# Moving the epsilon, the scale and the shift of four norms from GpSimd to VectorE in a two-layer vision tower

## The chip, the cores and the metric

The kernel runs on one core of one Trainium2 chip. The metric is device time in microseconds of one execution; the time given is the median of three runs. Engines are named as the profile names them: PE is TensorE's matmul, PEld its weight load, DVE is VectorE, ACT is ScalarE, POOL is GpSimd, SP is the queue that issues the transfers.

## The reference, cut to what matters

Thirty-two images of 3x96x96 become 37 tokens each (36 patches and a class token) of 256 numbers, 1184 tokens in all. Two layers follow, each with an attention-like part and a feed-forward part, and each part reads a layer norm of the residual `h`:

```
h = tok(x)                                             # patches @ W + b, class token, positions
h = h + minlstm(norm(h))                               # its own second norm, gates, scan over tokens, + its input
h = h + ffn(norm(h))                                   # ternary W_fc, gelu, norm over 1024, ternary W_proj
h = h + attention(norm(h))                             # rope, causal softmax, V and output weights
h = h + quant_linear(norm(h))                          # round(x / scale), clip, ternary weights
norm(h) = (h - mean) / sqrt(var + 1e-5)
```

The first part norms twice in a row; the kernel folds that into the powers of two numbers, `var + eps` and `var * (1 + eps) + eps * eps`. In the last part the normed value is divided by `scale = max(act_scale, 1e-5)` before rounding.

## The kernel before, in words

The 1184 tokens are cut into 11 tiles of three images, 111 rows each (74 in the last), one token to a partition. Each tile passes through the stages `tok`, `gate`/`scan`/`h1`, `fc`/`tg`/`proj`, `qk`/`value`/`score`/`attend`, and `t3`/`out`. `gate`, `scan`, `qk` and `rope` work on chunks of 4, 4 and 3 tiles. Matmuls in float32 are done as products of a high and a low part, so a PE result that is to be multiplied again is copied by ACT (high part) and subtracted by DVE (low part).

The order of work is written out by hand: the table `ORDER` holds for each engine a list of steps `stage:tile` (`stage:unit` for chunked stages), which the engine's program issues one after the other. Engines meet only at semaphores. The PSUM banks are handed out in the order of PE's list (`ring`), so moving a PE step also changes which earlier result a bank waits for. `NARROW`, with two banks, is shared by `w_pos`, `tok`, `h1`, `proj`, `value`, `score`, `attend`, `out` and some weight steps.

Each of the norms 0 to 3 of a tile is computed from one row of `small`, 35 numbers per token:

- DVE, `stats0` to `stats3` (L885): `bn_stats` of the 256 numbers of a row; `mean0` to `mean3` (L892): `bn_aggr`, giving mean and variance (`MV`), which raises `mv`.
- POOL, in its steps `h0` (norm 0), `h1` (norm 1), `proj` (norm 2) and `attend` (norm 3): `scaled` (L1181) computes `var + eps` into `VE`; norm 0 has two such instructions. `power` (L1186) raises to -0.5 into `R`, against the constant tile `powers`. Norm 3 multiplies by `1/scale` (L1272) into `RQ`. Norms 1 to 3 then have `shift` (L1191), which writes `-mean * R` into `NB`. Between any two of them POOL waits for its own semaphore. Norm 0's shift is already on DVE (L990).
- ACT, `n0` to `n3` (L729): `h * R + NB`. For norm 3 this is `s3`, which DVE clips (L1146) and rounds (L1154) and PE transposes (`t3`, L653) and multiplies (`out`, L664).

POOL's other work is: `split` (L1202, the low part of the input), `square` (the power of the 1024-wide norm, L1186 too), `hc`, `vbias` and `biased` (L1233, L1260, L1282, a 256-wide bias added to the residual), and `rope` (L1251). At the start SP issues the loads in the order input tile 0, `w_tok` in two halves, input tile 1, `pos_in` and `sel`, input tile 2 and so on; `w_pos` (L440) is the small matmul that needs `pos_in` and `sel`, and `warm` (L435) is a row of matmuls on ones.

Of the kernel before, what the change touches and what calls it, by code (L numbers as in the profile page):

```python
# [20 lines left out]
ALU = mybir.AluOpType  # L21
# [46 lines left out]
def chunk_of(i):  # L68
# [7 lines left out]
        warm:0 tok:0 w_pos:0 tok:1 tok:2 tok:3 w_gate:0 tok:4 t0:0 tok:5 t0:1 tok:6 t0:2 tok:7 w_fold:0 t0:3  # L76
        w_ternary:0 t0:4 w_fold:1 tok:8 tok:9 gate:0 gate:1 t0:5 w_value_bias:0 gate:2 gate:3 t0:6 tok:10 t0:7
        w_ln_bias:0 gate:4 gate:5 h1:0 gate:6 h1:1 t0:8 t0:9 h1:2 t0:10 gate:7 h1:3 t1:0 gate:8 gate:9 fc:0 t1:1
        fc:1 h1:4 gate:10 h1:5 h1:6 gate:11 h1:7 fc:2 t1:2 fc:3 t1:3 tg:0 fc:4 fc:5 tg:1 fc:6 fc:7 t1:4 tg:2
        tg:3 proj:0 h1:8 fc:8 t1:5 fc:9 tg:4 tg:5 fc:10 proj:1 h1:9 tg:6 fc:11 t1:6 t1:7 proj:2 h1:10 tg:7 fc:12  # L80
        tg:8 fc:13 tg:9 t2:0 fc:14 proj:3 t1:8 fc:15 tg:10 t2:1 tg:11 fc:16 proj:4 t2:2 tg:12 proj:5 t2:3 tg:13
        t1:9 fc:17 qk:0 qk:1 fc:18 tg:14 tg:15 proj:6 t1:10 qk:2 tg:16 qk:3 proj:7 t2:4 tg:17 fc:19 fc:20 t2:5
        value:0 t2:6 proj:8 fc:21 score:0 t2:7 tg:18 score:1 tg:19 qk:4 qk:5 score:2 turn:0 tg:20 proj:9 qk:6
        score:3 attend:0 tg:21 qk:7 value:1 turn:1 t2:8 proj:10 t2:9 value:2 attend:1 turn:2 value:3 score:4
        attend:2 turn:3 score:5 score:6 t2:10 attend:3 score:7 turn:4 qk:8 qk:9 qk:10 value:4 t3:0 turn:5
# [1272 lines left out]
```

## Time and profile before

| | us |
|---|---|
| median of 3 runs (163.96 to 165.28) | 164.39 |
| the profiled execution's own time | 163.71 |
| its span, first to last instruction | 161.9 |
| PE busy | 148.2 |
| DVE busy | 136.1 |
| POOL busy | 120.3 |
| ACT busy | 109.0 |

Times of rows are from the start of the span. Busy time is the union of an engine's instructions, and on PE an instruction's end is modelled, so PE can be "busy" over short waits. The profiled execution is 0.68 us under the median of the runs. The line numbers are those of the kernel before.

### The profile page before, as it was taken

To read this page: it belongs to the slowest core of one execution; us is meant where nothing else is said; L and a number is where in the kernel's file an instruction comes from. 1 tells how busy PE (TensorE), PEld (TensorE's weight loads), DVE (VectorE), ACT (ScalarE), POOL (GpSimd) and SP (SyncE) were. 2 spreads that over 40 slices of the span, in tenths; PEclk is the share of its full clock that TensorE was granted. 3 is DMA by queue.
4 is the path that set the end of the run, shared out by engine and by line. 5 is a ranking of instruction groups with operands and counts; after the bars stand their busy time and mean duration, and the time that the engine had idled before them with its cause. 6 is when DMAs were issued, how large, how long until landed. Compare 5 with 4: busy or idle time off the path is not lost.

```text
span 161.9 us, 3532 instructions
## 1 busy us (share of the span) xinstructions
PE 148.2 (91%) x1043; PEld 129.5 (80%) x1043; DVE 136.1 (84%) x396; ACT 109.0 (67%) x264; POOL 120.3 (74%) x214
## 2 busy tenths in 40 slices
PE   7979999999998999999999999999999999697541
PEld 7969999788997887879888989988998798574220
DVE  0767679999999999999979799888988896896871
ACT  3765359736448899999998958498827637276330
POOL 1068978968927466878889988869899888988830
PEclk9999999999999999999999999999999999999955
DMA  5999992000030000000000000000000000001323
GB/s 171 340 392 392 379 417 109 4 0 2 0 130 4 2 0 2 0 4 0 0 4 2 0 4 0 2 0 0 4 0 0 0 6 2 2 10 46 87 81 81
DMA packets 6026, 10.84 MB, mean 67 GB/s; under 512 B 1841, under 2 KB 3448, under 8 KB 5752
## 3 DMA queue, kind: packets, MB, share of 16 engines
q1 hardware_dynamic: 6008, 10.62, 18.7%
q8 instruction: 9, 0.15, 0.4%
q14 instruction: 9, 0.07, 0.2%
HBM read 9.40 MB, written 1.21 MB: 66 GB/s over the span
## 4 chain that ended last, share of the span: by engine, by line
PE 70%; POOL 13%; DVE 6%; issue 6%; ACT 2%; DVEq 0%; ACTq 0%; POOLq 0%
PE bank L428 37%; PE bank L508 5%; PE bank L575 5%; PE bank L509 4%; PE bank L510 4%; PE bank L517 3%; POOL small L1186 3%; PE bank L435 3%; POOL qk L1251 2%; POOL small L1181 2%; POOL residual L1282 2%; POOL small L1191 2%; PE bank L549 1%; PE bank L629 1%; DVE residual L1160 1%
## 5 line engine op out<-in xcount | busy, mean ns | idle before, releaser
L1186 POOL TENSOR_TENSOR small<-small,powers 111x1 f32<-111x1 f32 (+3 forms) x55 | 33.3, 606 | 3.7
L1181 POOL TENSOR_SCALAR small<-small 111x1 f32<-111x1 f32 (+1 forms) x55 | 24.2, 441 | 15.0 <-DVE small L892 11.3
L428 PE MATMUL bank<-pj,gt_hi 128*111 128x256 f32 (+1 forms) x88 | 22.3, 293 | 0.0
L428 PE MATMUL bank<-pj,gt_lo 128*111 128x256 f32 (+1 forms) x88 | 21.3, 281 | 0.0
L1202 POOL TENSOR_TENSOR x_lo<-x_raw,x_hi 128x666 fp32r<-128x666 f32 (+1 forms) x9 | 12.8, 1434 | 10.8 <-ACT x_hi L721 10.8
L508 PE MATMUL bank<-wt_hi,x_hi 128*111 128x256 f32 (+1 forms) x66 | 19.4, 294 | 1.4 <-DVE h L998 1.1
L510 PE MATMUL bank<-wt_hi,x_lo 128*111 128x256 f32 (+1 forms) x66 | 18.6, 282 | 0.0
L509 PE MATMUL bank<-wt_lo,x_hi 128*111 128x256 f32 (+1 forms) x66 | 18.6, 282 | 0.0
L428 PE MATMUL bank<-fc,n1t_hi 128*111 128x512 f16 (+1 forms) x44 | 16.7, 380 | 0.0
L428 PE MATMUL bank<-fc,n1t_lo 128*111 128x512 f16 (+1 forms) x44 | 16.6, 378 | 0.0
L428 PEld LDWEIGHTS bank<-pj,gt_hi 128*111 128x111 f32 (+1 forms) x88 | 15.1, 171 | 0.3 <-DVE residual L1088 0.2
L428 PEld LDWEIGHTS bank<-pj,gt_lo 128*111 128x111 f32 (+1 forms) x88 | 15.1, 171 | 0.1
L815 ACT ACTIVATE gt_hi<-bank 128x444 fp32r<-128x444 f32 (+1 forms) x22 | 11.7, 537 | 4.4 <-PE bank L575 4.2
L1111 DVE SCALAR_TENSOR_TENSOR rope<-bank,packed,consts 128x444 f32<-128x444 f32 (+1 forms) x24 | 13.4, 621 | 1.2 <-PE bank L428 1.1
L1071 DVE SCALAR_TENSOR_TENSOR gw<-g,small,ln_w 111x1024 f32<-111x1024 f32 (+1 forms) x11 | 14.3, 1296 | 0.0
L897 DVE TENSOR_TENSOR gt_lo<-bank,gt_hi 128x444 fp32r<-128x444 f32 (+1 forms) x22 | 13.1, 596 | 1.2 <-ACT gt_hi L815 1.2
L885 DVE BATCH_NORM_STATS2 stats<-residual 111x6 f32<-111x256 f32 (+1 forms) x33 | 13.9, 420 | 0.2
L729 ACT ACTIVATE n<-residual,small 111x256 f32<-111x256 f32 (+1 forms) x22 | 13.3, 604 | 0.6 <-POOL small L1191 0.6
L508 PEld LDWEIGHTS bank<-wt_hi,x_hi 128*111 128x111 f32 (+1 forms) x66 | 11.5, 174 | 2.6 <-DVE h L998 1.5
L1251 POOL TENSOR_TENSOR qk<-rope 128x444 f32<-128x444 f32 (+1 forms) x12 | 13.0, 1108 | 0.7 <-DVE rope L1111 0.5
L795 ACT ACTIVATE g<-bank 111x512 f32<-111x512 f32 (+1 forms) x22 | 13.1, 605 | 0.4 <-PE bank L428 0.3
L1191 POOL TENSOR_SCALAR small<-small 111x1 f32<-111x1 f32 (+1 forms) x33 | 10.7, 325 | 3.4
(139 smaller groups left out, 478.9 us busy)
## 6 DMA issues: line engine op xcount, KB each, us to landing
x_raw<-x_in SPq DMA_DIRECT2D x10, 333.0 KB, 6.4
w_fc<-w_fc_in SPq DMA_DIRECT2D x1, 1024.0 KB, 10.2
w_pj<-w_pj_in SPq DMA_DIRECT2D x1, 1024.0 KB, 12.2
out_dram<-residual SPq DMA_DIRECT2D x10, 96.0 KB, 1.7
w_tok<-w_tok_in SPq DMA_DIRECT2D x2, 384.0 KB, 4.1
w_gate<-w_gate_in SPq DMA_DIRECT2D x1, 512.0 KB, 5.8
w_qk<-w_qk_in SPq DMA_DIRECT2D x1, 512.0 KB, 7.0
ln_w<-ln_w_in SPq DMA_DIRECT2D x1, 512.0 KB, 3.5
```

The costliest lines, as they stand in the source:

```text
L428: last = mm(out, a, b, start=(n == 0), stop=(n == len(pairs) - 1))
L508: mm(out[0:n, 0:D], hi, wt_hi[:, k, :], start=(k == 0), stop=False)
L509: mm(out[0:n, 0:D], hi, wt_lo[:, k, :], start=False, stop=False)
L510: last = mm(out[0:n, 0:D], lo, wt_hi[:, k, :], start=False, stop=(k == KX - 1))
L729: return go(out, h[0:n, i, :], ACT.Identity, scale=small[0:n, i, factor:factor + 1], bias=small[0:n, i, shift:shift + 1])
L885: nc.vector.bn_stats(stats[0:n, norm, i % 2, 0:6], h[0:n, i, :]).then_inc(s[f"stats{norm}_ready"], 1)
L1071: stt(out=gw[0:n, i % 2, :], in0=g[0:n, i % 2, :], scalar=col(i, MVG), in1=ln_w[0:n, :], op0=ALU.subtract, op1=ALU.mult).then_inc(s["gw_re ...
L1111: last = stt(out=rope[:, t, 0:width].rearrange("p (m t) -> p m t", t=T), in0=banks[WIDE[("qk", 4 * c + b)][0]][:, 0:width].rearrange("p (m ...
L1181: return nc.gpsimd.tensor_scalar(small[0:rows(i), i, out:out + 1], small[0:rows(i), i, value:value + 1], factor, add, ALU.mult, ALU.add)
L1186: return gt(small[0:rows(i), i, r:r + n], small[0:rows(i), i, ve:ve + n], powers[0:rows(i), 0:n], ALU.pow)
L1191: nc.gpsimd.tensor_scalar(small[0:rows(i), i, nb:nb + 1], small[0:rows(i), i, mv:mv + 1], small[0:rows(i), i, r:r + 1], -1.0, ALU.mult, AL ...
L1251: gt(qk[:, 2 * j + part, cs], rope[:, t, 0:width], rope[:, t + 1, 0:width], op)\
```

## The change

On DVE, `mean0` to `mean3` get a second part: after `bn_aggr` they wait for its own semaphore and compute `VE` (two instructions for norm 0, one for norms 1 and 2). For norm 3 the one instruction computes `(var + eps) * scale^2`, so the power gives `R/scale` directly; the multiplication by `1/scale` is gone, and the reciprocal in `w_small` becomes a square. New DVE stages `nb1`, `nb2`, `nb3` wait for POOL's power and compute `NB`. POOL's steps `h0`, `h1`, `proj` and `attend` keep one instruction each, the power. `ORDER` is written anew for all four engines.

```diff
+EPS_ON_VECTOR = (0, 1, 2, 3)
+NB_ON_VECTOR = (1, 2, 3)
...
     "tensor": """
-        warm:0 tok:0 w_pos:0 tok:1 tok:2 tok:3 w_gate:0 tok:4 t0:0 tok:5 t0:1 tok:6 t0:2 tok:7 w_fold:0 t0:3
+        warm:0 w_pos:0 tok:0 tok:1 tok:2 tok:3 w_gate:0 t0:0 tok:4 t0:1 tok:5 tok:6 w_fold:0 t0:2 tok:7
...
# DVE, mean_of(norm)
                     nc.vector.bn_aggr(col(i, normed[norm][2], 2), stats[0:rows(i), norm, i % 2, 0:6])\
                         .then_inc(s[f"mv{norm}_ready"], 1)
+                    dve.wait_ge(s[f"mv{norm}_ready"], i + 1)
+                    mv, ve = normed[norm][2], (VE0, VE1, VE2, VE3)[norm]
+                    if norm == 3:
+                        if i == 0:
+                            dve.wait_ge(s["sq_scale_ready"], 1)
+                        ts(col(i, ve), col(i, mv + 1), LN_EPS, derived[0:rows(i), D_SQ_SCALE:D_SQ_SCALE + 1], ALU.add,
+                           ALU.mult).then_inc(s["ve3_ready"], 1)
+                    elif norm in EPS_ON_VECTOR:
+                        ts(col(i, ve), col(i, mv + 1), 1.0, LN_EPS, ALU.mult, ALU.add).then_inc(s[f"ve{norm}_ready"], 1)
+                    if norm == 0 and norm in EPS_ON_VECTOR:
+                        ts(col(i, ve + 1), col(i, mv + 1), 1.0 + LN_EPS, LN_EPS * LN_EPS, ALU.mult, ALU.add)\
+                            .then_inc(s["ve0_ready"], 1)
+            def nb_of(norm):
+                def stage(i):
+                    r = (R0, R1, R2, RQ)[norm]
+                    dve.wait_ge(s[("r0_ready", "r1_ready", "r2_ready", "rq_ready")[norm]], i + 1)
+                    ts(col(i, (NB0, NB1, NB2, NB3)[norm]), col(i, normed[norm][2]), col(i, r), -1.0, ALU.mult, ALU.mult)\
+                        .then_inc(s[f"nb{norm}_ready"], 1)
+                return stage
...
# POOL
             def attend(i):
                 n = rows(i)
-                pool.wait_ge(s["mv3_ready"], i + 1)
-                scaled(i, VE3, MV3 + 1, 1.0, LN_EPS).then_inc(s["ve3_ready"], 1)
                 pool.wait_ge(s["ve3_ready"], i + 1)
-                power(i, VE3, R3).then_inc(s["r3_ready"], 1)
-                if i == 0:
-                    pool.wait_ge(s["inv_scale_ready"], 1)
-
-                pool.wait_ge(s["r3_ready"], i + 1)
-                gt(small[0:rows(i), i, RQ:RQ + 1], small[0:rows(i), i, R3:R3 + 1],
-                   derived[0:rows(i), D_INV_SCALE:D_INV_SCALE + 1], ALU.mult).then_inc(s["rq_ready"], 1)
-                pool.wait_ge(s["rq_ready"], i + 1)
-                shift(i, NB3, MV3, RQ, "nb3_ready")
+                power(i, VE3, RQ).then_inc(s["rq_ready"], 1)
```

How the order moves is shown at three places. The first is POOL near the end of the program, around the norm 3 of tiles 7 and 8, before the change (L1181 is the epsilon, L1186 the power, L1272 the scale, L1191 the shift, L1282 the bias):

```order
L1181 TENSOR_SCALAR small<-small 111x1 [waits mv3_ready]
L1186 TENSOR_TENSOR small<-small,powers 111x1 [waits ve3_ready]
L1272 TENSOR_TENSOR small<-small,derived 111x1 [waits r3_ready]
L1191 TENSOR_SCALAR small<-small 111x1 [waits rq_ready]
L1181 TENSOR_SCALAR small<-small 111x1 [waits mv3_ready]
L1186 TENSOR_TENSOR small<-small,powers 111x1 [waits ve3_ready]
L1272 TENSOR_TENSOR small<-small,derived 111x1 [waits r3_ready]
L1191 TENSOR_SCALAR small<-small 111x1 [waits rq_ready]
L1282 TENSOR_TENSOR residual<-residual,out_bias 111x256 [waits s3_ready] x2
```

and the same place with the change, where L1208 is the power and L1277 the bias:

```order
L1208 TENSOR_TENSOR small<-small,powers 111x1 [waits ve3_ready] x2
L1277 TENSOR_TENSOR residual<-residual,out_bias 111x256 [waits s3_ready]
L1208 TENSOR_TENSOR small<-small,powers 111x1 [waits ve3_ready]
L1277 TENSOR_TENSOR residual<-residual,out_bias 111x256 [waits s3_ready] x3
L1208 TENSOR_TENSOR small<-small,powers 111x1 [waits ve3_ready]
```

Four instructions per tile have become one, and the bias instructions stand between them. The second place is DVE in the feed-forward part, around norm 1 of tile 6. Before (L1071 is the product with `ln_w`, L897 a low part, L1040 the scan, L1056 and L1060 the mean and variance of the 1024-wide norm):

```order
L1071 SCALAR_TENSOR_TENSOR gw<-g,small,ln_w 111x1024 [waits mvg_ready]
L897 TENSOR_TENSOR gt_lo<-bank,gt_hi 128x444 [waits gt_hi_ready]
L1056 TENSOR_SCALAR small<-small 111x1 [waits g_ready]
L897 TENSOR_TENSOR gt_lo<-bank,gt_hi 128x444 [waits gt_hi_ready]
L892 BN_AGGR small<-stats 111x2 [waits stats1_ready]
L1040 SCALAR_TENSOR_TENSOR hs<-keep,zc 128x296 [waits keep_ready,zc_ready] x2
L1060 TENSOR_SCALAR small<-small 111x1 [waits squares_ready] x2
```

With the change (L922 is the low part, L896 `bn_aggr`, L906 the epsilon, L1072 the residual of `h1`, L917 the shift, L1096 the product with `ln_w`):

```order
L922 TENSOR_TENSOR gt_lo<-bank,gt_hi 128x444 [waits gt_hi_ready] x2
L896 BN_AGGR small<-stats 111x2 [waits stats1_ready]
L906 TENSOR_SCALAR small<-small 111x1 [waits mv1_ready]
L1072 TENSOR_TENSOR residual<-bank,residual 111x256 [waits res0_ready,pe_hs]
L922 TENSOR_TENSOR gt_lo<-bank,gt_hi 128x444 [waits gt_hi_ready]
L917 TENSOR_SCALAR small<-small 111x1 [waits r1_ready]
L1096 SCALAR_TENSOR_TENSOR gw<-g,small,ln_w 111x1024 [waits pe_tg,mvg_ready]
```

The epsilon stands right behind the `bn_aggr` that it waits for, and the shift two instructions later, behind which the 1024-wide product is queued. The third place is PE's start, before:

```order
L435 MATMUL bank<-ones 128x128 x10
L508 MATMUL bank<-wt_hi,x_hi 111x256 [waits wt_lo_ready,wt_hi_ready,x01_lo_ready]
L509 MATMUL bank<-wt_lo,x_hi 111x256
L510 MATMUL bank<-wt_hi,x_lo 111x256
...
L440 MATMUL bank<-pos_in,sel 111x256 [waits dma_pos]
L508 MATMUL bank<-wt_hi,x_hi 111x256 [waits x01_lo_ready,x_hi_ready,h0_ready]
```

and with the change:

```order
L439 MATMUL bank<-ones 128x128 x10
L444 MATMUL bank<-pos_in,sel 111x256 [waits dma_pos]
L512 MATMUL bank<-wt_hi,x_hi 111x256 [waits wt_lo_ready,wt_hi_ready,x01_lo_ready]
L513 MATMUL bank<-wt_lo,x_hi 111x256
L514 MATMUL bank<-wt_hi,x_lo 111x256
```

`w_pos` now stands ahead of `tok:0`, and waits there for `pos_in` and `sel`. The bank of `tok:1` is then that of `w_pos` and no longer that of `tok:0`.

## Rows read from the trace of the kernel before

**Rows 1.** The page's first part: busy us, share of the span, instructions.

```profile
PE 148.2 (91%) x1043; PEld 129.5 (80%) x1043; DVE 136.1 (84%) x396; ACT 109.0 (67%) x264; POOL 120.3 (74%) x214
```

**Rows 2.** By stretch: bounds, length, busy PE, PEld, DVE, ACT, POOL; PEclk, DMA share, GB/s.

```profile
35.00:80.00 45.00, 44.57 (x307) 38.90 (x306) 44.64 (x117) 36.56 (x86) 32.91 (x56) 1.00 0.04 13
80.00:112.00 32.00, 32.00 (x240) 28.39 (x238) 28.07 (x71) 25.65 (x64) 27.73 (x48) 1.00 0.01 2
112.00:151.00 39.00, 35.65 (x249) 29.92 (x247) 33.20 (x127) 22.09 (x69) 33.78 (x71) 1.00 0.03 7
```

**Rows 3.** The page's chain that ended last, by engine.

```profile
PE 70%; POOL 13%; DVE 6%; issue 6%; ACT 2%; DVEq 0%; ACTq 0%; POOLq 0%
```

**Rows 4.** Waits of the whole run: total us, times, longest.

```profile
POOL small L1181 <- DVE small L892: 11.3, 11, 2.7
ACT s L729 <- POOL small L1191: 1.8, 1, 1.8
```

**Rows 5.** PE's timeline in the feed-forward part: start and duration in us.

```profile
62.12 0.38 PE L428 MATMUL bank<-fc,n1t_hi 128*111 128x512 f16 x1
...
63.63 0.38 PE L428 MATMUL bank<-fc,n1t_lo 128*111 128x512 f16 x1
```

**Rows 6.** Line L892 (`bn_aggr`) alone, by stretch: busy us and count.

```profile
35.00:80.00 45.00, 2.54 (x15) 1.00 0.04 13
80.00:112.00 32.00, 1.24 (x7) 1.00 0.01 2
112.00:151.00 39.00, 2.28 (x13) 1.00 0.03 7
```

**Rows 7.** DVE's small instructions by form: count, busy us, mean ns, idle before.

```profile
L1056 DVE TENSOR_SCALAR small<-small 111x1 f32<-111x1 f32 x10 | 2.0, 200 | 0.0
L1128 DVE TENSOR_SCALAR small<-small 111x1 f32<-111x1 f32 x10 | 1.4, 142 | 0.0
```

**Rows 8.** DVE's timeline: how soon the next instruction starts.

```profile
141.66 0.15 DVE L1128 TENSOR_SCALAR small<-small 111x1 f32<-111x1 f32 x1
141.73 0.17 DVE L892 BATCH_NORM_AGGREGATE small<-stats 111x2 f32<-111x6 f32 x1
141.82 0.27 DVE L1154 TENSOR_SCALAR q<-s 111x256 f16<-111x256 f32 x1
...
13.87 0.14 DVE L939 TENSOR_SCALAR derived<-packed 128x1 f32<-128x1 f32 x1
14.05 0.16 DVE L942 RECIPROCAL derived<-derived 128x1 f32<-128x1 f32 x1
...
70.82 0.20 DVE L1056 TENSOR_SCALAR small<-small 111x1 f32<-111x1 f32 x1
70.94 0.41 DVE L885 BATCH_NORM_STATS2 stats<-residual 111x6 f32<-111x256 f32 x1
```

**Rows 9.** The last tile's norm 3, from DVE's and POOL's timelines.

```profile
151.33 0.17 DVE L892 BATCH_NORM_AGGREGATE small<-stats 74x2 f32<-74x6 f32 x1
...
152.56 0.19 POOL L1181 TENSOR_SCALAR small<-small 74x1 f32<-74x1 f32 x1
152.82 0.55 POOL L1186 TENSOR_TENSOR small<-small,powers 74x1 f32<-74x1 f32 x1
...
153.74 0.26 POOL L1191 TENSOR_SCALAR small<-small 74x1 f32<-74x1 f32 x1
```

**Rows 10.** The start: warm matmuls, input tile 1 landed, `w_pos`, `tok:1`.

```profile
1.04 5.06 PE L435 MATMUL bank<-ones 128*128 128x128 f32 x22 [1.04 <-DVE ones L906]
...
7.58 0.86 ACT L688 ACTIVATE x_hi<-x_raw 128x333 fp32r<-128x333 f32 x2 [0.54 <-DMA x_raw<-x_in]
...
9.05 0.68 PE L440 MATMUL bank<-pos_in,sel 39*111 39x256 f32 x2
...
10.79 0.37 PE L508 MATMUL bank<-wt_hi,x_hi 128*111 128x256 f32 x1 [1.05 <-DVE h L998]
```

**Rows 11.** The last stretch, columns as in rows 2.

```profile
154.00:161.90 7.90, 2.37 (x10) 1.16 (x10) 3.34 (x8) 1.29 (x4) 1.40 (x3) 0.50 0.30 83
```

More of the change, by code:

```diff
@@ L75 @@
     "tensor": """
-        warm:0 tok:0 w_pos:0 tok:1 tok:2 tok:3 w_gate:0 tok:4 t0:0 tok:5 t0:1 tok:6 t0:2 tok:7 w_fold:0 t0:3
[L77 to L85, printed above, removed]
@@ new lines @@
+        w_ternary:0 w_fold:1 t0:3 tok:8 gate:0 gate:1 gate:2 t0:4 t0:5 gate:3 t0:6 tok:9 w_ln_bias:0 t0:7
+        w_value_bias:0 tok:10 h1:0 gate:4 h1:1 gate:5 h1:2 gate:6 t0:8 gate:7 t0:9 t0:10 h1:3 t1:0 t1:1 gate:8
+        gate:9 fc:0 gate:10 fc:1 t1:2 h1:4 h1:5 gate:11 fc:2 h1:6 h1:7 fc:3 t1:3 fc:4 t1:4 fc:5 tg:0 fc:6 tg:1
+        fc:7 fc:8 tg:2 fc:9 t1:5 tg:3 h1:8 proj:0 tg:4 fc:10 t1:6 tg:5 fc:11 proj:1 fc:12 fc:13 tg:6 tg:7 h1:9
+        proj:2 tg:8 t1:7 h1:10 tg:9 proj:3 fc:14 tg:10 fc:15 tg:11 t1:8 proj:4 t2:0 t2:1 proj:5 t1:9 fc:16 fc:17
@@ new lines @@
+        t2:2 tg:12 t2:3 value:0 fc:18 tg:13 qk:0 qk:1 tg:14 proj:6 t1:10 qk:2 tg:15 qk:3 fc:19 tg:16 t2:4 tg:17
+        proj:7 fc:20 t2:5 fc:21 t2:6 score:0 proj:8 t2:7 score:1 tg:18 tg:19 qk:4 score:2 qk:5 turn:0 tg:20
+        tg:21 proj:9 attend:0 qk:6 qk:7 value:1 proj:10 turn:1 score:3 t2:8 attend:1 turn:2 value:2 score:4
+        score:5 turn:3 attend:2 value:3 turn:4 score:6 turn:5 value:4 attend:3 t2:9 value:5 attend:4 t2:10
+        attend:5 t3:0 value:6 score:7 qk:8 qk:9 turn:6 value:7 attend:6 turn:7 qk:10 attend:7 qk:11 value:8 t3:1
@@ new lines @@
+    "gpsimd": """
+        w_tok:0 split:3 h0:0 split:4 split:5 h0:1 split:6 split:7 h0:2 split:8 h0:3 split:9 h0:4 split:10 h0:5
+        h0:6 h0:7 split:11 h0:8 h0:9 h1:0 h0:10 h1:1 hc:0 h1:2 hc:1 h1:3 h1:4 h1:5 h1:6 square:0 h1:7 square:1
+        hc:2 square:2 hc:3 h1:8 proj:0 square:3 hc:4 proj:1 h1:9 hc:5 proj:2 square:4 vbias:0 vbias:1 proj:3
+        vbias:2 square:5 hc:6 h1:10 vbias:3 proj:4 hc:7 hc:8 proj:5 square:6 rope:0 proj:6 square:7 vbias:4
+        rope:1 proj:7 square:8 proj:8 hc:9 vbias:5 square:9 vbias:6 hc:10 rope:2 square:10 attend:0 vbias:7
+        vbias:8 rope:3 proj:9 proj:10 attend:1 vbias:9 attend:2 biased:0 attend:3 biased:1 biased:2 attend:4
+        vbias:10 rope:4 biased:3 attend:5 biased:4 rope:5 attend:6 attend:7 biased:5 attend:8 biased:6 biased:7
+        biased:8 attend:9 attend:10 biased:9 biased:10""",
@@ L941, in w_small @@
                 dve.wait_ge(s["scale_ready"], 1)
-                nc.vector.reciprocal(derived[:, D_INV_SCALE:D_INV_SCALE + 1], derived[:, D_SCALE:D_SCALE + 1])\
-                    .then_inc(s["inv_scale_ready"], 1)
+                ts(derived[:, D_SQ_SCALE:D_SQ_SCALE + 1], derived[:, D_SCALE:D_SCALE + 1],
+                   derived[:, D_SCALE:D_SCALE + 1], None, ALU.mult).then_inc(s["sq_scale_ready"], 1)
             def w_qk_(_i):
@@ L1170, in _ @@
                       "clip": clip, "round": round_, "out": out_}
+            stages |= {f"nb{norm}": nb_of(norm) for norm in NB_ON_VECTOR}
             for norm in range(4):
@@ L1178, in _ @@
             gt = nc.gpsimd.tensor_tensor
-            def scaled(i, out, value, factor, add):
-                return nc.gpsimd.tensor_scalar(small[0:rows(i), i, out:out + 1], small[0:rows(i), i, value:value + 1],
-                                               factor, add, ALU.mult, ALU.add)
             def power(i, ve, r, n=1):
@@ L1187, in power @@
                           ALU.pow)
-            def shift(i, nb, mv, r, ready):
-                nc.gpsimd.tensor_scalar(small[0:rows(i), i, nb:nb + 1], small[0:rows(i), i, mv:mv + 1],
-                                        small[0:rows(i), i, r:r + 1], -1.0, ALU.mult, ALU.mult).then_inc(s[ready], 1)
             def w_tok_(_i):
```

106 lines of the change are left out of this document (44 added, 62 removed).

## The prediction

> **What bounds the kernel now.** I read the page's busy times first. PE is busy for 148.2 us, DVE for 136.1 and POOL for 120.3 of a span of 161.9 [rows 1]: three engines are near the whole, so work taken from one and put on another is not free by itself. Busy shares are averages, so I next cut the span into stretches [rows 2]. From 35 to 80 us, the second half of the gates and the first half of the feed-forward part, PE is busy for 44.57 of 45 us and DVE for 44.64: both are full. From 80 to 112 us PE is busy for all 32 us and DVE for 28.07, which leaves DVE 3.93 us. From 112 to 151 us, where attention and the quantized layer overlap, PE leaves 3.35 us of 39, DVE 5.80 and POOL 5.22.
>
> PE's busy time can hide short waits, so I looked at its starts. Eight matmuls of 512 columns start from 62.12 to 63.63 us, 0.216 us apart though each is shown as 0.38 long [rows 5]. They follow each other without a gap: in the full stretches PE really works, and no relief of POOL can make it faster there. The chain that ended last says the same, with 70% on PE and 13%, some 21 us, on POOL [rows 3]. The POOL part lies after 112 us. Among the waits, POOL's longest is 11.3 us for DVE's `bn_aggr`, which is POOL waiting and not being waited for. What waits for POOL's shift is little: ACT's `s3` once, for 1.8 us [rows 4].
>
> So POOL's small instructions cost time in the last 50 us, and DVE has no room in the 45 us in the middle. The change takes from the first and puts onto the second.
>
> **The change part by part.** *What leaves POOL.* Per tile one epsilon for norms 1 to 3 and two for norm 0, three shifts and one scale: 55 + 33 + 11 = 99 instructions, of which I price only what is waited for. In the last tile the four instructions of norm 3 run from 152.56 to 154.00 us, and 0.55 of these 1.44 us is the power, which stays [rows 9].
>
> *What DVE gains.* 55 instructions for `VE` and 33 for `NB`. DVE has tiny instructions of both kinds. One without a pointer operand (L1128) is 142 ns long, and one that takes a second column as its scalar, as `NB` and norm 3's `VE` do, is 200 ns (L1056) [rows 7]. What they take from DVE is less, since the next instruction starts early: behind L1128 after 0.07 us, and behind L1056 after 0.12 [rows 8]. I take 0.065 and 0.12. Then there is the new wait of DVE for itself. Behind a `bn_aggr` the next instruction starts after 0.09 us, but the new one needs its result. In the pair L939 and L942, where the second needs the first, it starts 0.04 us after the end of the first; the `bn_aggr` of 0.17 us then costs 0.21, that is 0.12 more [rows 8]. So a mean step grows by 0.12 + 0.065 = 0.18 us for norms 1 and 2, by 0.12 + 0.12 = 0.24 for norm 3, and by 0.12 + 2 x 0.065 = 0.25 for norm 0; each `nb` adds 0.12. Over the run that is 11 x 0.25 + 22 x 0.30 + 11 x 0.36 = 13.3 us, a tenth of DVE's work.
>
> Here a rule can be weighed. By the rows above, DVE starts an instruction while the one before it is still shown as running, so an added one costs 0.065 or 0.12 us. The Trainium skill, "VectorE: DVE Perf Modes", section "The DRAIN you can't avoid", says that the next operation does not start until the pipeline of the last one is empty. Taken as written that would charge each instruction its whole length, 44 x 0.142 + 44 x 0.200 = 15.0 us before any wait of DVE for itself. The starts in rows 8 speak for the smaller price, and I use it.
>
> *Middle, 35 to 112 us.* It holds 22 of the 44 `bn_aggr` [rows 6]. By the order the first 8 of norm 0 lie before 35 us, so 3 of the 22 are of norm 0 and 19 of norms 1 and 2: 3 x 0.25 + 12 x 0.30 = 4.35 us more on DVE up to 80 us, and 7 x 0.30 = 2.1 up to 112. DVE's idle time there is 0.36 and 3.93 us [rows 2]. If the new order used every idle moment, the excess would be 6.45 - 4.29 = 2.2 us. If nothing can be carried from the first stretch to the second, where PE is full and every delay stays, and the `nb` waits cost their own price there, it is 4.0 + 2.1 = 6.1 us. I take 3.0, near the lower end, because low parts and 1024-wide statistics are queued some tiles ahead of their use, and the new order does move them.
>
> *Tail, 112 to 151 us.* DVE gains 3 x 0.30 + 10 x 0.36 = 4.5 us against 5.8 idle, and PE has 3.35 us idle [rows 2, 6]. POOL loses some ten times 0.9 us of four-instruction chains. What shrinks is limited by PE to 3.35 us, and by DVE's remaining room to 1.3 us unless work moves. I take 1.5.
>
> *Last tile.* From `bn_aggr` at 151.33 us to the end of the shift at 154.00 are 2.67 us, of which 1.06 is POOL's queue before L1181 [rows 9]. The new path is 0.21 for `bn_aggr` and its wait, 0.20, the power's 0.55, 0.20 for the shift, and some 0.1 us on each way between the engines (POOL's steps in rows 9 lie 0.07 us apart): 1.4 us. I take 1.2 us of gain, between nothing (if the output steps of DVE and PE end last anyway) and 1.3.
>
> *Start.* `w_pos` now stands ahead of `tok:0`, which ran at once before. Its inputs are queued behind input tile 1, which landed at 7.58 us, and had landed by 9.05 [rows 10]. If they land at 8.0, `w_pos` (0.68) ends near 8.6. `tok:0` is 18 matmuls of 256 columns, half of the width that takes 0.216 us in rows 5, and two small warm ones, some 2.4 us, and ends near 11.1. `tok:1` follows at once, because its bank no longer waits for `h0:0`; that wait was 1.05 us, and `tok:1` started at 10.79 [rows 10]. So PE is 0.3 us later, between -0.1 and +1.4. The additions before 35 us, 8 x 0.25 = 2 us, lie in DVE's idle time (136.1 less the three stretches of rows 2 leaves it busy for 30.2 of the 45.9 us before 35 and after 151): nothing. If that cover fails they cost up to 2 us. The reciprocal that becomes a product costs nothing either way: each is one instruction of 0.2 us.
>
> The sum is 0.3 + 3.0 - 1.5 - 1.2 = +0.6 us on the profiled execution's 163.71, so 164.3. The median of the runs stands 0.68 above that execution, so the forecast for the median is 164.39 + 0.6 = **165.0 us**. A change of less than 1% (162.7 to 166.0) is about what a measurement of this kernel cannot tell from none.
>
> **The rivals.** *A, the forecast: the middle pays a little more than the tail returns.* For it: PE without gaps and DVE at 99% in the middle, POOL with its small instructions on the chain in the tail. 165.0 us, chance 0.35. Its own range is 163.4 to 166.6.
>
> *B, the tail returns more.* POOL's relief is used up to PE's idle time, 3.35 + 1.3 = 4.7 us, and the middle costs 1.0 because DVE work slides past 112 us. +0.3 + 1.0 - 4.7 = -3.4, so 161.0 us. For it: POOL is busy 33.78 of 39 us there, and its queue delays each norm 3 behind a bias [rows 2, 9]. Against it: DVE must then work almost without a pause. Chance 0.28.
>
> *C, DVE becomes the bound of the feed-forward part.* Per tile DVE gains two mean steps and two shifts, 0.60 us, and PE nothing. Where DVE was full already, each tile's low part comes later and PE waits for it. The place is 35 to 112 us, the price 6.1 us, and it decides as soon as less than about 2 us of DVE work can be moved out of the stretch before 80 us. +0.3 + 6.1 - 2.7 = +3.7, so 168.1 us. A shift that waits for POOL's power has a product of 1.3 us queued behind it, and makes this worse. The same page of the Trainium skill, section "Rules for kernel authors", advises to minimize the number of operations, since each has a fixed cost; on a full DVE this is that rule. Chance 0.26.
>
> *D, the clock falls at the start.* Between the warm matmuls, which end at 6.1 us [rows 10], and `w_pos` near 8.0, PE now idles. At the end of the run, where PE is busy for only 2.37 of 7.9 us, the granted clock is 0.50, 1.2 GHz [rows 11]. If `tok:0` ran at half speed it would take 2.1 us more: 165.0 + 2.1 = 167.1 us. Against it: 5 us of unbroken matmuls stand just before. Chance 0.06.
>
> *E, the change does nothing for the time.* PE's own work sets the pace, and both DVE's additions and POOL's relief are hidden: 164.39 + 0.3 = 164.7 us. Against it: DVE's full stretch. Chance 0.05.
>
> **How the numbers follow.** Faster by over 1% is B, 0.28. Slower by over 1% is C and D, 0.32. Within 1% is A and E, 0.40. The range reaches down to B and up to just past C: 160.9 to 168.6 us, which leaves out the lower part of B and the upper part of C, some 0.2 together.
>
> **What would show each step.** DVE's busy time near 148 us, with `bn_aggr` followed 0.21 us later by its epsilon, would confirm the price; POOL's busy time should be near 85 us. The middle is right if PE's step `fc:21` and its neighbours come 2 to 4 us later than before and PE shows waits for DVE's low parts. The tail is right if the stretch from the first `score` to the end is shorter, and the last norm 3 takes 1.4 us from `bn_aggr` to the shift. The start is right if `w_pos` starts near 8.0 us and `tok:1` follows `tok:0` without a wait. The prediction fails if DVE turns out to have slack in the middle that its busy time hides, or if the new order's tail is better packed than a sum over stretches can see.

## The result: 3.4% slower, just outside the range

The changed kernel takes 169.31 us (median of 4 runs, 168.18 to 170.20), the kernel before beside it 164.18 (4 runs). The ratio is 1.034, 95% interval 1.030 to 1.038. The forecast was 165.0 us with a range up to 168.6. Times are medians of all executions; the ratios leave out an execution that lies over 1.5% above the fastest of its kernel, so a median and its ratio can differ by some tenths of a us. The profiled execution took 169.06 us with a span of 167.3, against 163.71 and 161.9.

The page of the changed kernel, busy times, and its chain that ended last, by engine:

```profile
PE 151.8 (91%) x1043; PEld 132.6 (79%) x1043; DVE 146.3 (87%) x484; ACT 108.3 (65%) x264; POOL 88.0 (53%) x115
...
PE 57%; DVE 23%; POOL 7%; issue 6%; DMA 3%; ACT 2%; SPq 1%; DVEq 0%; POOLq 0%
```

The instructions moved as told: POOL fell from 120.3 to 88.0 us (forecast near 85), DVE rose from 136.1 to 146.3 (forecast near 148) [rows 1]. POOL's part of the chain halved, from 13% to 7%, but DVE's rose from 6% to 23% [rows 3]. The stretches of [rows 2], and the first 35 us (bounds, length, busy PE, PEld, DVE, ACT, POOL; granted clock, DMA share, GB/s):

```profile
0.00:20.00 20.00, 15.83 (x84) 14.65 (x85) 9.41 (x22) 9.42 (x17) 5.85 (x10) 1.00 0.94 332
20.00:35.00 15.00, 14.27 (x116) 13.50 (x114) 12.58 (x47) 8.89 (x14) 10.72 (x8) 1.00 0.37 150
35.00:80.00 45.00, 43.66 (x286) 37.23 (x287) 44.27 (x135) 32.90 (x78) 15.78 (x19) 1.00 0.04 13
80.00:112.00 32.00, 32.00 (x239) 28.57 (x238) 31.30 (x93) 26.15 (x65) 22.71 (x32) 1.00 0.01 2
112.00:151.00 39.00, 37.27 (x277) 33.30 (x276) 37.36 (x145) 23.98 (x71) 26.48 (x37) 1.00 0.03 7
```

DVE is now full to 112 us: 31.30 of 32 us where it was 28.07. To see where the time went I took the starts of the same steps from PE's timeline, each step's first matmul. The last column is what the rest of this text explains.

```
step      before   change   later by
tok:1      10.79    13.81     3.0
tok:3      15.14    19.71     4.6
gate:4     46.39    53.15     6.8
fc:0       55.16    62.24     7.1
proj:10   121.56   128.09     6.5
attend:10 149.04   155.50     6.5
out:10    158.05   163.07     5.0
```

All of the loss is there at 62 us, before the feed-forward part begins. The first 4.6 us arise in the first 20. The stretch from 35 to 112 us was to pay 3.0 us, but from `fc:0` on nothing more is paid, and 1.1 us come back behind `attend:10` (the span ends 5.4 us later than before). The order moves a few steps across these marks: ahead of `fc:0` PE now has `t1:1` as well, and `score:3`, `t2:8` and `turn:1`, small ones, stand behind `proj:10` instead of ahead of it.

**The start.** PE's timeline of the changed kernel: start, duration, and in brackets the idle time before and what ended it.

```profile
7.87 1.19 PE L444 MATMUL bank<-pos_in,sel 39*111 39x256 f32 x2 [1.75 <-DMA sel<-sel_in]
8.98 0.55 PE L512 MATMUL bank<-wt_hi,x_hi 128*111 128x256 f32 x1
...
9.76 0.41 PE L512 MATMUL bank<-wt_hi,x_hi 128*111 128x256 f32 x1
9.97 0.41 PE L513 MATMUL bank<-wt_lo,x_hi 128*111 128x256 f32 x1
...
14.03 0.29 PE L513 MATMUL bank<-wt_lo,x_hi 128*111 128x256 f32 x1
14.15 0.28 PE L514 MATMUL bank<-wt_hi,x_lo 128*111 128x256 f32 x1
14.27 0.28 PE L512 MATMUL bank<-wt_hi,x_hi 128*111 128x256 f32 x1
...
19.71 0.37 PE L512 MATMUL bank<-wt_hi,x_hi 128*111 128x256 f32 x1 [1.37 <-DVE h L1023]
```

PE waits 1.75 us for the DMA of `sel`. Then the matmuls of `tok:0` start 0.21 us apart, and from 14.03 us on 0.12 us apart, a factor of 1.8. `w_pos` shows it too: 1.19 us for what took 0.68 before [rows 10]. The granted clock of this run reads 1.00 there, but in experiments 2 and 3, where `tok:0` has the same spacing, it reads 0.50 from 10 to 12 us, that is 1.2 GHz against 2.4. The page's row of the granted clock cuts the span into 40 slices of 4.2 us; here it is for the changed kernel and then for experiment 2, whose third slice falls to 6 tenths:

```profile
PEclk9999999999999999999999999999999999999855
PEclk9969999999999999999999999999999999987965
```

`tok:3`, the last line above, waits another 1.37 us for DVE's residual of `tok:1`. What DVE did in that time comes next.

**DVE beside POOL.** DVE's timeline of the first norm 0, and POOL's low part of the input at the same time:

```profile
14.98 0.18 DVE L896 BATCH_NORM_AGGREGATE small<-stats 111x2 f32<-111x6 f32 x1
15.20 0.15 DVE L906 TENSOR_SCALAR small<-small 111x1 f32<-111x1 f32 x1
15.27 0.14 DVE L908 TENSOR_SCALAR small<-small 111x1 f32<-111x1 f32 x1
16.30 2.63 DVE L1015 SCALAR_TENSOR_TENSOR small<-small 111x1 f32<-111x1 f32 x1 [0.90 <-POOL small L1208]
18.86 0.14 DVE L1034 TENSOR_SCALAR small<-small 111x1 f32<-111x1 f32 x1
```

```profile
16.24 2.69 POOL L1219 TENSOR_TENSOR x_lo<-x_raw,x_hi 128x666 fp32r<-128x666 f32 x2
```

Two readings. The price of the moved instructions is as forecast: `bn_aggr` to epsilon 0.22 us (0.21 taken), epsilon to the next 0.07. But norm 0's shift, one column, 0.15 us elsewhere, is shown for 2.63 us and ends at 18.93, the moment at which POOL's two subtractions end. The residuals of `tok:1` and `tok:2` are queued behind it on DVE and start at 19.25, and `tok:3` follows at 19.71. So of the 4.6 us that `tok:3` is late, 3.0 are there at `tok:1` and 1.6 come from this queue.

### The profile page after: what moved, and what is told of

The parts are those of the page before. It is cut to its first block, busy times and chain, and to the rows that moved or that the text cites. A ratio compares the mean times of both kernels' runs of the same rounds, so it can differ in the third digit from the quotient of the medians.

```text
span 167.3 us, 3521 instructions
## 1 busy us (share of the span) xinstructions
PE 151.8 (91%) x1043; PEld 132.6 (79%) x1043; DVE 146.3 (87%) x484; ACT 108.3 (65%) x264; POOL 88.0 (53%) x115
## 4 chain that ended last, share of the span: by engine, by line
PE 57%; DVE 23%; POOL 7%; issue 6%; DMA 3%; ACT 2%; SPq 1%; DVEq 0%; POOLq 0%
PE bank L432 33%; PE bank L579 5%; POOL qk L1256 3%; DVE small L1015 3%; DMA sel<-sel_in 3%; PE bank L521 3%; DVE stats L889 2%; PE bank L633 2%; PE bank L648 2%; PE bank L512 2%; PE bank L668 2%; DVE rope L1136 2%; DVE n L1026 2%; POOL small L1208 2%; PE bank L514 2%
## 5 line engine op out<-in xcount | busy, mean ns | idle before, releaser
L1208 POOL TENSOR_TENSOR small<-small,powers 111x1 f32<-111x1 f32 (+3 forms) x55 | 38.1, 698 | 48.4 <-DVE small L906 24.1
L1219 POOL TENSOR_TENSOR x_lo<-x_raw,x_hi 128x666 fp32r<-128x666 f32 (+1 forms) x9 | 14.1, 1570 | 17.0 <-ACT x_hi L725 17.0
L512 PE MATMUL bank<-wt_hi,x_hi 128*111 128x256 f32 (+1 forms) x66 | 20.2, 306 | 1.4 <-DVE h L1023 1.4
L513 PE MATMUL bank<-wt_lo,x_hi 128*111 128x256 f32 (+1 forms) x66 | 19.3, 293 | 0.0
L514 PE MATMUL bank<-wt_hi,x_lo 128*111 128x256 f32 (+1 forms) x66 | 19.3, 293 | 0.0
L512 PEld LDWEIGHTS bank<-wt_hi,x_hi 128*111 128x111 f32 (+1 forms) x66 | 12.1, 184 | 2.9 <-DVE h L1023 1.9
L1096 DVE SCALAR_TENSOR_TENSOR gw<-g,small,ln_w 111x1024 f32<-111x1024 f32 (+1 forms) x11 | 14.0, 1275 | 0.0
L922 DVE TENSOR_TENSOR gt_lo<-bank,gt_hi 128x444 fp32r<-128x444 f32 (+1 forms) x22 | 13.0, 594 | 0.0
L808 ACT ACTIVATE squares<-g,small 111x1024 f16<-111x1024 f32 (+1 forms) x11 | 12.7, 1155 | 0.1
L513 PEld LDWEIGHTS bank<-wt_lo,x_hi 128*111 128x111 f32 (+1 forms) x66 | 12.2, 185 | 0.0
```

The costliest lines, as they stand in the source:

```text
L512: mm(out[0:n, 0:D], hi, wt_hi[:, k, :], start=(k == 0), stop=False)
L513: mm(out[0:n, 0:D], hi, wt_lo[:, k, :], start=False, stop=False)
L514: last = mm(out[0:n, 0:D], lo, wt_hi[:, k, :], start=False, stop=(k == KX - 1))
L1096: stt(out=gw[0:n, i % 2, :], in0=g[0:n, i % 2, :], scalar=col(i, MVG), in1=ln_w[0:n, :], op0=ALU.subtract, op1=ALU.mult).then_inc(s["gw_re ...
L1208: return gt(small[0:rows(i), i, r:r + n], small[0:rows(i), i, ve:ve + n], powers[0:rows(i), 0:n], ALU.pow)
L1219: gt(x_lo[:, i, :, 0:n], x_raw[:, i, :, 0:n], x_hi[:, i % X_SLOTS, :, 0:n].bitcast(F32), ALU.subtract).then_inc(s["x_lo_ready"], 1)
```

## Experiments

Every ratio is against the kernel before, run beside it on the same chip.

**1. `tok:0` ahead of `w_pos:0` again.**

```diff
-        warm:0 w_pos:0 tok:0 tok:1 tok:2 tok:3
+        warm:0 tok:0 w_pos:0 tok:1 tok:2 tok:3
```

> The changed kernel with one step moved on PE: tok:0 before w_pos:0, as in the kernel before. Theory START: the changed kernel lost about 3 us by the end of tok:1 (13.81 us against 10.79) because w_pos waited until 7.87 us for its input and tok:0 then ran at the lower clock (0.213 us per matmul of 256 columns against 0.118). With tok:0 first it should start near 6.0, run at 0.118, and tok:1 should start near 10.8; if that delay is carried to the end, the time falls by about 3 us, to 166.3. Theory DVE LOAD: the 13.3 us of additions on DVE set the first 60 us whatever PE does at the start; the 3 us are lost again in a wait for DVE by the first fc, and the time stays above 168.5.

167.11 us, ratio 1.016 (1.005 to 1.027). `tok:3` starts at 15.32 us instead of 19.71: the half speed is gone, and so is the long shift (0.16 us at 12.75). So 2.2 us of the 5.1 hang on this one swap by the medians, 2.9 by the ratios. START is borne out for that part only. `fc:0` is still 3.3 us later than in the kernel before (58.44 us), although `tok:3` is only 0.2 late.

**2. More warm matmuls ahead of `w_pos`.**

```diff
-WARM = 11
+WARM = 16
```

> The changed kernel with 16 warm matmuls for 11, so that PE does not idle before w_pos. It separates the clock from the wait. If PE's clock fell in the idle time (although the profile grants 1.00 there), tok:0's matmuls come back to 0.118 us apart, tok:1 starts near 11.7 instead of 13.8, and the time falls by about 2 us, to 167.2. If the 0.213 us have another cause, they stay, and the time is unchanged or 0.5 us longer, 169.3 to 169.8.

167.95 us, ratio 1.022 (1.011 to 1.033). The run did not do what it was meant to. `w_pos` started only at 8.66 us, because `sel` came later than in the changed kernel's trace (7.87), so PE still idled for 1.50 us. `w_pos` takes 0.68 us again, but `tok:0` then runs at half speed until 12.6 us, where the changed kernel did until 14.0. `tok:1` starts 0.3 us earlier and the span is 0.4 us shorter. The medians differ by 1.4 us, but the intervals of the two ratios overlap. So whether warm matmuls up to `w_pos` would keep the clock was not tried; what the run shows is the granted clock of 0.50 beside the spacing of 0.21 us.

**3. Norm 0's shift with a pointer instead of a second tensor.**

```diff
-    return stt(out=col(i, nb), in0=col(i, mv), scalar=-1.0, in1=col(i, r), op0=ALU.mult, op1=ALU.mult)
+    return ts(col(i, nb), col(i, mv), col(i, r), -1.0, ALU.mult, ALU.mult)
```

> The changed kernel with norm 0's shift as a tensor_scalar (one tensor and a pointer) and not a scalar_tensor_tensor of two columns. Theory PORT: the shift of tile 0 took 2.63 us and that of tile 2 1.59 us, each until POOL's x_lo ended, because a DVE instruction with two SBUF tensors waits for POOL's; as a tensor_scalar it takes 0.2 us, tok:3 (which waits for DVE's h0:1) comes about 2.4 us earlier, and the time falls by 1.5 to 2.5 us, to about 167.3. Rival: what waits is any small instruction while POOL works, or the record is only long; then the new form is as long and the time stays at 169.3.

169.01 us, ratio 1.032 (1.024 to 1.039): nothing gained, and `tok:3` still waits 1.17 us for DVE. DVE, then POOL at the same time:

```profile
15.54 0.21 DVE L1015 TENSOR_SCALAR small<-small 111x1 f32<-111x1 f32 x1 [0.90 <-POOL small L1207]
15.67 0.14 DVE L1033 TENSOR_SCALAR small<-small 111x1 f32<-111x1 f32 x1
15.73 2.57 DVE L1025 TENSOR_SCALAR n<-h,small 111x256 f32<-111x256 f32 x1
```

```profile
15.47 2.68 POOL L1218 TENSOR_TENSOR x_lo<-x_raw,x_hi 128x666 fp32r<-128x666 f32 x2
```

The shift now passes in 0.21 us, and the wide product two instructions later takes the wait: 2.57 us for what is 0.40 elsewhere. The stall belongs to the time at which DVE meets POOL's subtraction, and changing the form hands it to the next instruction that is open to it.

**4. Both of these.**

> Both edits of the two kernels before together. If START and PORT are two causes in a row on one path, their gains add: 169.3 - 3.0 - 2.0 = 164.3, level with the kernel before. If they overlap (the shift's wait fills time that PE would have waited anyway), about 166. If DVE LOAD holds, above 167.5.

166.53 us, ratio 1.017 (1.006 to 1.028), the same as the first alone. Some 2.5 us against the kernel before (2.8 by the ratio) remain that neither explains.

**5. The new orders with the old arithmetic** (the `nb` steps left out of DVE's list).

> The new orders of all four engines with the old arithmetic (epsilons and shifts stay on GpSimd, no nb steps). Of the 5.1 us that the change cost (164.2 to 169.3), the first four runs gave 2.2 to 2.8 back when tok:0 went ahead of w_pos:0 again. Theory ORDER (the order's start costs, the moved instructions are nearly free): 168 to 169 us, tok:3 some 4 us and fc:0 some 6 us later than before. Theory LOAD (VectorE is busy without a gap from about 25 us to 80 us in both kernels, so what is added to it ahead of 60 us is paid one for one: 11 x (0.21 + 0.07) for norm 0 and about 3 tiles of norm 1 ahead of fc:0, 3.5 us): the order alone costs only its start, 166.5 us. A third possibility, that the order was laid out so as to need the moved instructions, gives over 170 us, because GpSimd has 120 us of work and the order asks for its results sooner.

178.39 us, ratio 1.089 (1.082 to 1.096): the third possibility. The order has `w_pos:0` first, so the price of the start is in it. The waits of this run (us in total, times, longest):

```profile
POOL small L1181 <- DVE small L892: 28.8, 12, 5.7
...
ACT n L729 <- POOL small L1191: 5.4, 5, 1.4
DVE small L990 <- POOL small L1186: 5.0, 6, 1.5
```

The new order asks for POOL's results sooner than POOL can give them with its old work. It is no better order in itself; it fits the moved instructions.

**6. The kernel before with `w_pos:0` ahead of `tok:0`**, and nothing else.

```diff
-        warm:0 tok:0 w_pos:0 tok:1 tok:2 tok:3
+        warm:0 w_pos:0 tok:0 tok:1 tok:2 tok:3
```

> The kernel before with one step moved: w_pos:0 ahead of tok:0 on the tensor engine. It takes out all else, so it prices the step that the prediction put at +0.3. From the trace of the change (tok:1 3.0 us later) and the first runs (2.2 us back): 166.3 us, with tok:1 2.5 to 3 us later. Rival: VectorE is full from 25 us on and most of the loss of the start is taken up in its idle time before that (3.9 us of waits before 20 us), then the time is 164 to 165 us.

166.75 us, ratio 1.017 (1.010 to 1.024): +2.6 us for a swap that was priced at +0.3. Its profile shows the same half speed:

```profile
8.90 1.19 PE L440 MATMUL bank<-pos_in,sel 39*111 39x256 f32 x2 [3.68 <-DVE wt_lo L897]
10.02 0.55 PE L508 MATMUL bank<-wt_hi,x_hi 128*111 128x256 f32 x1
...
10.80 0.41 PE L508 MATMUL bank<-wt_hi,x_hi 128*111 128x256 f32 x1
11.02 0.41 PE L509 MATMUL bank<-wt_lo,x_hi 128*111 128x256 f32 x1
```

The granted clock reads 0.50 from 8 to 14 us. The delay is carried unchanged: in this execution `tok:3` is 4.2 us later, `fc:0` 4.3 and `out:10` 4.3. (The profiled execution is the longest of its four; `w_pos` starts only at 8.90 us.) Nothing later absorbs a late start, so the rival expectation falls. How late `sel` comes differs between executions: `w_pos` starts at 7.87 us in the changed kernel's trace, at 8.27 in experiment 3, at 8.66 in experiment 2 and at 8.90 here.

**7. Norm 3 alone moved, in the order of before**, each `nb3` two to four steps behind its `mean3`.

> The kernel before, with norm 3 alone moved: epsilon times scale squared and shift on VectorE, GpSimd keeps its power; norms 0, 1 and 2 stay on GpSimd; the order is that of before with the eleven nb3 steps put in two to four behind their mean. If the tail is what the move buys (prediction: -1.5 in the tail and -1.2 on the last tile), this gives it without the price of the start and of the full VectorE: 161.5 to 162.5 us. If VectorE's additions in the tail (11 x 0.45 us = 5 us, of which half stands beside waits) eat it: 163.5 to 164.5 us.

164.67 us, ratio 1.003 (0.999 to 1.008): no change. `score:8` starts 1.1 us later than before, `out:4` 1.3, `out:10` 0.7, of which 0.6 were there at `tok:1`. The tail pays 0.7 us and the last tile returns 0.6. The relief of POOL in the tail, on its own and with these places of `nb3`, buys nothing.

**8. All four norms moved, in the order of before**, each `nb` three steps behind its mean (norm 3: two to four).

> The new arithmetic of all four norms in the orders of the kernel before; each nb step stands three steps of VectorE behind the mean of its tile (two to four in norm 3). w_pos ahead of tok:0, which alone cost 2.6 us (166.75 against 164.13), is not in it. Theory LOAD (what is added to a full VectorE is paid): 165.5 to 167 us, fc:0 some 3 us later than before. Theory ORDER (all of what is left of the loss, 2.5 us, comes from how the other steps were laid out anew): 163.5 to 164.5 us.

175.29 us, ratio 1.070 (1.065 to 1.075): +11.45 us, some four times the most that either theory expected. Where the `nb3` steps stand is narrow: with most of them a step earlier the engines wait for each other in a circle and the program never ends. In the changed kernel the distance from mean to `nb` is not fixed; it goes from 2 to 14 steps. **9.** and **10.** split it: norm 0 alone, and norms 1 and 2 alone, by the same means.

> The kernel before with norm 0 alone moved: its two epsilons on VectorE (11 x 0.28 us by the rows of the changed kernel), its power on GpSimd; norms 1, 2 and 3 as before. LOAD: ten of the eleven tiles lie ahead of fc:0 and VectorE is full from 25 us on; some four tiles fall in its idle time before that, so 11 x 0.28 less 4 x 0.28 = 2 us: 166 us. ORDER: GpSimd's 2 x 0.27 us of each tile leave the way from the mean to the power, which buys as much back: 164 us.

> The kernel before with norms 1 and 2 alone moved: epsilon (0.21 with its wait for the aggregate) and shift (0.12 from start to start) on VectorE for 22 tiles, 7 us of VectorE's time between 45 and 125 us; norms 0 and 3 as before. The prediction put +3.0 on the stretch from 35 to 112 us for norms 0, 1 and 2 together. LOAD: three tiles ahead of fc:0, 1 us, and the feed-forward part on PE (32.00 of 32 us busy) hides the others: 165 to 165.5 us. Rival that VectorE bounds the feed-forward part too: 7 us less the 3 that are idle from 80 to 112 us, 168 us. ORDER: 164 us.

Norm 0 alone 167.31 us, ratio 1.021 (1.017 to 1.025); norms 1 and 2 alone 171.23 us, ratio 1.047 (1.042 to 1.052). With norm 3 of experiment 7 the parts are 3.5 + 7.4 + 0.5 = 11.4 us, and the whole was 11.45: they add up, in the order of before.

*Norm 0.* DVE, POOL and PE of that run:

```profile
27.50 2.09 DVE L1009 SCALAR_TENSOR_TENSOR small<-small 111x1 f32<-111x1 f32 x1
...
29.58 0.40 DVE L1020 TENSOR_SCALAR n<-h,small 111x256 f32<-111x256 f32 x1
```

```profile
27.34 0.69 POOL L1211 TENSOR_TENSOR small<-small,powers 111x2 f32<-111x2 f32 x1 [1.64 <-DVE small L902]
27.99 1.59 POOL L1222 TENSOR_TENSOR x_lo<-x_raw,x_hi 128x666 fp32r<-128x666 f32 x1
```

```profile
30.04 0.41 PE L519 MATMUL bank<-consts,n 111*128 111x111 f32 x2 [1.06 <-DVE n L1020]
31.44 0.38 PE L478 MATMUL bank<-derived,ones 128*128 128x2 f32 x2 [1.00 <-DVE h L1017]
...
33.86 0.41 PE L511 MATMUL bank<-wt_lo,x_hi 128*111 128x256 f32 x1
34.07 0.41 PE L512 MATMUL bank<-wt_hi,x_lo 128*111 128x256 f32 x1
...
36.63 0.32 PE L512 MATMUL bank<-wt_hi,x_lo 128*111 128x256 f32 x1
36.79 0.28 PE L510 MATMUL bank<-wt_hi,x_hi 128*111 128x256 f32 x1
```

With its two small instructions fewer, POOL starts this subtraction at 27.99 us, where it started at 29.50 before, and it now falls on DVE's shift, which ends with it at 29.59. PE waits for the product behind the shift, then for `h0`, and its matmuls from 33.86 to 36.63 us start 0.21 us apart. Here the page's granted clock shows it, in its ninth slice (33.0 to 37.1 us):

```profile
PEclk9999999959999999999999999999999999999955
```

Neither the changed kernel nor experiment 1 has such a second slow stretch. At `fc:0` this run is 3.3 us later than before (58.49 us), at `out:10` 3.0.

*Norms 1 and 2.* `fc:0` starts at 55.34 us, 0.2 later than before; `fc:21` at 114.04, 4.7 later; `t2:10` at 135.12, 6.5 later. The loss grows through the feed-forward part, and with 7.4 us it is nearly twice the 4.2 of the rival expectation. Its chain from 60 us on (start, length, what), and the stretch from 80 to 112:

```profile
60.07 0.95 DVE zc L1051 x2
61.02 1.19 DVE gw L1092
...
63.37 0.20 DVE small L913
63.57 0.33 DVE residual L1068
63.90 0.29 DVE n1t_lo L918
64.19 0.10 DVE small L896
64.39 0.21 DVE small L1077
```

```profile
80.00:112.00 32.00, 29.95 (x212) 25.41 (x210) 29.15 (x84) 23.44 (x59) 21.15 (x26) 1.00 0.01 2
```

From 60 to 83 us the chain is on DVE but for one power of POOL (0.6 us), where before it was on PE. Then PE, which was busy for all 32 us [rows 2], loses 2.05.

**11. The changed kernel with `tok:0` first and norm 0's epsilons back on GpSimd.**

> The changed kernel with tok:0 ahead of w_pos:0 again (which gave 2.2 us back) and, beside that, norm 0's two epsilons back on GpSimd; norms 1, 2 and 3 and all the rest of the new orders stay. In the orders of before, moving norm 0 alone cost 3.5 us (167.31 against 163.84). If that price stands in the new order as well (theory START: the additions ahead of 35 us), the time is 164 to 165 us. If the new order needs norm 0's results as early as it now gets them (the order with the old arithmetic was 14.3 us slower than before), GpSimd's 0.5 us per tile come back on the way and it stays at 167 us or goes over it.

168.41 us, ratio 1.030 (1.021 to 1.038). Against the 167.11 us of experiment 1 nothing came back; if anything 1.3 us were lost (the intervals overlap). `fc:0` starts at 60.20 us against 58.44 there. The 3.5 us of norm 0 are the price in the old order and can't be taken out of the new one. Theory START falls, the other expectation holds.

**12. Norms 1 and 2 as in experiment 10, each `nb` six steps behind its mean instead of three.**

> The kernel before with norms 1 and 2 alone moved, as in the run that took 171.23 us, but with each nb step six steps of VectorE behind its mean instead of three. Theory LOAD (the 7 us of instructions are paid because VectorE bounds the feed-forward part in this order): 170.5 to 171.5 us, no change. Theory PLACE (VectorE stood 3.0 us at nb steps for GpSimd's power, and ScalarE 3.3 us for nb): it gives 2 to 4 us of the 7.4 back, 167 to 169 us; if the later nb makes ScalarE's norm late instead, over 172 us.

172.80 us, ratio 1.051 (1.044 to 1.058), the last of the expectations. DVE no longer waits for the power, and ScalarE waits instead:

```profile
ACT n L733 <- DVE small L913: 11.0, 10, 2.3
```

In experiment 10 that wait was 3.3 us in 3 times, beside DVE's own 3.0. So neither of the two fixed distances is the better one: what DVE gains ScalarE loses. A distance chosen tile by tile, as in the changed kernel, was not tried in this order.

## Why the prediction was wrong

The forecast's terms beside what the two traces show. Each measured number is the growth of the delay between two starts on PE:

| stretch | forecast | measured |
|---|---|---|
| up to `tok:1` | +0.3 | +3.0 |
| `tok:1` to `tok:3` | 0 | +1.6 |
| `tok:3` to `fc:0` (15 to 55 us) | 0 up to 35 us, then part of +3.0 | +2.5 |
| `fc:0` to `proj:10` | the rest of +3.0 | -0.6 |
| `proj:10` to `attend:10` | -1.5 | -0.1 |
| `attend:10` to the end | -1.2 | -1.1 |
| sum, of the unrounded numbers | +0.6 | +5.4 |

**The start, priced at +0.3 us, is the step that failed.** The estimate of `w_pos` near 8.0 us was right (7.87), and so was `tok:1` directly behind `tok:0`. What was wrong is `tok:0` itself: taken as 2.4 us, measured 4.8 from 8.98 to 13.81. Some 0.6 us of the difference could be seen beforehand: in the kernel before `tok:0` lies between the warm matmuls' end at 6.1 us and `w_pos` at 9.05 [rows 10], 3.0 us and not 2.4. The other 1.8 us, with 0.4 in `w_pos`, are the half speed. That is rival D, whose price of +2.1 us was good and whose chance of 0.06 was not. The only ground against it was that 5 us of matmuls stand just before. In the changed kernel 1.75 us of idle time stood between them and the matmuls at 1.2 GHz; in experiment 3, after 2.16 us, `w_pos` and the first three matmuls of `tok:0` still ran at full speed and the next ones did not. The kernel before has an idle time of 1.05 us at 9.7 us and no slow matmul behind it. The single swap measured +2.6 us in the kernel before, and its withdrawal 2.2 (2.9 by the ratios) in the changed one.

**A term was missing: DVE's wait beside POOL.** The forecast had no price for it, and it makes the 1.6 us from `tok:1` to `tok:3`. It hangs on the start, since in experiment 1 the shift takes 0.16 us again.

**The additions before 35 us, priced at nothing, failed at least in the order of before.** I had set 2 us of them against DVE's idle time in the first 35 us as a sum. But in the kernel before DVE is busy for 10.66 of the 15 us from 10 to 25, where its idle time is waits for PE and ACT, and for 9.70 of the 10 us from 25 to 35, which gives no cover. There norm 0 alone costs 3.5 us. The bound "if that cover fails up to 2 us" was too low as well. It counted the instructions, and not that faster steps on POOL move its subtraction onto DVE's path, nor that PE's waits bring the low clock. For the changed kernel this is not shown. In experiment 1 `fc:0` is 3.3 us late, about half of it by `tok:8` near 33 us, but with norm 0's epsilons taken off DVE (experiment 11) it is 5.0 us late. So what makes the loss between `tok:3` and `fc:0` in the new order stays open.

**The middle, +3.0: the price of the instructions right, the sum not.** The instructions cost what was worked out (0.22 and 0.07 us where 0.21 and 0.065 were taken). Rival C, with 6.1 us for the middle, is what happens in the order of before: norms 1 and 2 alone, 22 x 0.30 = 6.6 us of DVE's work, cost 7.4. In the new order the feed-forward part pays nothing: `fc:21` is 4.8 us late (with `proj:8` and `t2:6` now behind it) and `proj:10` 6.5, more than the 2 to 4 us that the prediction gave as its sign, but `fc:0` was late by 7.1 already. Between all norms moved in the old order (+11.45 us) and the changed kernel with `tok:0` first (1.016, +2.6 us) lie 8.8 us that belong to the rest of the order, the places of the `nb` steps included. I had let it move at most 4 us. Most of it lies between `fc:0` and `proj:10`: 72.83 us in the run of experiment 8, 65.86 in experiment 1, 65.85 in the changed kernel and 66.40 in the kernel before. Which of its moves do it was not tried. That the chain runs on PE there again, with DVE at 31.30 of 32 us, shows that DVE's idle time from 80 to 112 us was used to the end, as the lower bound of the middle had assumed.

**The tail, -1.5, did not come; the last tile, -1.2, did.** From `proj:10` to `attend:10` the changed kernel gains 0.1 us, and from there to the end 1.1. The last norm 3 in DVE's timeline of the changed kernel:

```profile
157.67 0.17 DVE L896 BATCH_NORM_AGGREGATE small<-stats 74x2 f32<-74x6 f32 x1
157.88 0.21 DVE L903 TENSOR_SCALAR small<-small,derived 74x1 f32<-74x1 f32 x1
...
159.31 0.20 DVE L917 TENSOR_SCALAR small<-small 74x1 f32<-74x1 f32 x1
```

1.84 us from `bn_aggr` to the end of the shift, against 2.67 [rows 9] and the 1.4 forecast: the shift started 0.6 us after POOL's power had ended, behind a rounding and an output step of DVE. From that `bn_aggr` to the end of the span it is 9.6 us, against 10.6 before. Experiment 7 shows no gain of the tail by itself either. Rival B, the tail returning 4.7 us, is not what happened.

**The sum.** The swap of one step, tried both ways, shows the start as 2.2 to 2.9 us of the 5.1. What is left arises between `tok:3` and `fc:0` (+2.5 us in the trace, +3.1 in experiment 1), less 1.7 us that come back later, and no run shows its cause. That the terms of the prediction don't stand one by one is shown: with the same additions one order gives +11.45 us and another +5.1. A split of the order's 8.8 us stays open, and so does whether experiment 11 lost 1.3 us or nothing.

No version beat the kernel before. The nearest is norm 3 alone, which is the same within its interval.

## What to carry to other kernels

Price a swap in a start-up order by what PE does while it waits: here an idle time of 1.75 us behind warm-up matmuls was followed by 5 us of matmuls at half speed, which cost another 2 us, and the delay was carried to the end. Sum an engine's idle time only over the stretch in which the added work must run; idle time spent in waits for another engine early on is no cover for additions later. And when instructions move together with an order laid out for them, try both alone: here the order alone (with its start) cost 14.3 us, the move alone 11.45, and the two together 5.1, so neither term of a prediction stands without the other.

## What the runs showed of the hardware

- The granted clock can read 1.00 while PE runs at half speed. In the changed kernel the stretch from 0 to 20 us has 1.00 although its matmuls from 8.98 to 13.8 us are 0.21 us apart; the same half speed in experiment 2 stands as 0.91, and as 0.50 from 10 to 12 us. The spacing of equal matmuls shows it in both.
- While POOL subtracts two tensors of 128x666 (mostly 1.36 to 1.63 us each), some DVE instructions wait until it ends, in the changed kernel through two subtractions in a row (2.69 us): a one-column product of two tensors (2.63 us for 0.15), a product of 111x256 with pointers (2.57 for 0.40). One-column instructions with a pointer or a constant passed in 0.21 and 0.14 us beside it. The kernel before had such stalls too, on `w_fc`'s cut (3.15 us at 30.37, against 1.28 in the changed kernel), and there PE waited only 0.3 and 0.4 us at 30 and 34 us.
